# Two layers of a graph network on one core: six buffers for second sigmoids in place of four, nine late load entries in place of ten

## The chip, the cores and the metric

The kernel runs on one core of one Trainium2 chip. The core has five engines that run their own lists of instructions and wait for one another by semaphores: TensorE (PE in the profile; its weight loads are PEld), VectorE (DVE), ScalarE (ACT), GpSimd (POOL) and SyncE (SP), which here issues the loads and stores. The metric is the device time of the program in microseconds, lower is better. The kernel before took 2234.77 us as the median of three runs (2233.01 to 2239.25).

## The reference

`x` is 8192 x 128 and `adj` is 8192 x 8192, all in f32. Layer 0 averages over neighbours; layer 1 weighs every entry of `adj` and of its transpose with a sigmoid of its own:

```python
# layer 0
A = a * adj, with (1 - a) added on the diagonal
x = layernorm(x + relu((A @ x) / A.sum(1) @ W.T + b))
# layer 1
xt  = logmap0(x)
par = adj   * sigmoid((xt @ w_par[:d])[:, None] + (xt @ w_par[d:])[None, :] + b_par)
chi = adj.T * sigmoid((xt @ w_chi[:d])[:, None] + (xt @ w_chi[d:])[None, :] + b_chi)
x = layernorm(x + proj(expmap0(chi @ xt + par @ xt)))
```

Each 8192 x 8192 matrix of scores is thus made once entry by entry, multiplied with `adj`, and consumed by a matmul; none is stored.

## The kernel before, in words

The output is cut into eight panels of 1024 rows. Layer 0 reads `adj` turned, in 256 pairs of tiles (a pair is 128 x 2048, 1 MB), and sums up TensorE products of them. Layer 1 is cut into 512 **units**. Unit n belongs to one panel and one tile of 128 neighbours; it works on 128 x 1024 elements:

- ScalarE makes two sigmoids: the second one, `chi(n)`, into SBUF (L720), and then the first one into a PSUM slot (L737), of which there are three in turn.
- GpSimd multiplies `chi(n)` in place by half of a loaded entry, "nat" (L537, `second_product`).
- VectorE multiplies the PSUM slot by half of another entry, "trn" (L986, `first_product`), and adds the two products into one of three `keys` buffers (L995, `key`).
- TensorE multiplies the keys with the tangent `xtA` (two matmuls of 512 columns, L1180) and sums over the panel's units.

154 units run early, among layer 0's pairs. The other 358 form the **late stage**, which this change touches. Two kinds of units differ there. In an **apart** unit (set `APART`: the unit numbers with n % 8 == 2) the addition is left out: VectorE's product goes straight to `keys`, and TensorE multiplies `keys` (L1180) and `chi` (L1186) one after the other. The buffer of `chi` is then free only when TensorE is done with it, while in all other units it is free when VectorE's addition has read it. In an **own** unit (eight in a row for each of the five panels that end in the late stage) the second matrix is not loaded: TensorE turns the "nat" entries (L1196), and these entries are held until all eight own units are turned.

The order on every engine is written out unit by unit. After a panel's last unit its **final steps** are laid among the next units at fixed distances b + F_...: ScalarE takes out the sums (L760) and squares them (L771), TensorE sums the squares into norms (L1205, just ahead of unit b + 4), ScalarE takes their root (L776; this needs one table load before and one after, because the sigmoids' table is another) ahead of unit b + 7, small steps follow on GpSimd and VectorE, and from b + 14 on ScalarE normalises the panel before, one eighth in each unit (L793). Such steps start at the units 232, 266, 304, 338, 376, 410 and 448; one more root (L781) stands ahead of unit 482.

**Buffers for chi.** `buffer_of` gives three buffers until unit 184 (`MORE`), and from then on four, the fourth in a part of `xA` that layer 0 no longer needs. So `chi(n)` waits until unit n - 4 has let go of its buffer: for `k_ready` (VectorE's addition), or behind an apart unit for `kt_used` (TensorE). The first sigmoid of unit n waits for its PSUM slot, which unit n - 3 held.

**Entries for loads.** SyncE loads 1 MB entries into a ring of seven, and from unit 160 on of ten: three more (`EXTRA`) lie in `xA`. The entries go round in turn, so load i waits for what load i - 10 brought: a "nat" entry is free after GpSimd's second product of the two units, a "trn" entry after VectorE's first product of the two.

Round in this text means the stretch from one own unit to the same one of the next panel, by VectorE's first products: round A is 1493.95 to 1679.68 us, B to 1864.92, C to 2050.11, D (64 units; the others have 72) to 2210.14.

Of the kernel before, what the change touches and what calls it, by code (L numbers as in the profile page):

```python
# [13 lines left out]
BP = 1024  # L14
# [14 lines left out]
CH = 2 * BP  # L29
# [2 lines left out]
PAIRS = NPAN * PPP  # L32
EARLY = 3
RING = 7
EXTRA = 3
CB = 3
KB = 3
SB = 3
PE_LAG = 2
# [133 lines left out]
def load_plan():  # L173
# [10 lines left out]
    for i, (kind, j) in enumerate(kinds):  # L184
        if i == late + RING - 1:
            entries = list(range(RING, RING + EXTRA)) + entries
        e = entries.pop(0)
# [68 lines left out]
MORE = LATE0 + 30  # L256


def buffer_of(n, few):

    if n < MORE:
        return n % few, n - few if n >= few else None
    k = (n - MORE) % (few + 1)
    return (few, n - few - 1 if n > MORE else None) if k == 0 else ((MORE + k - 1) % few, n - few - 1)

# [10 lines left out]
def adj_resnorm_kernel(nc, x_g, xT, g_blk, a_blk, WT, b_row, alpha, w_par, b_par, w_chi, b_chi, out):  # L278
    with ExitStack() as ctx:
        def sb(name, shape):  # L280
            return ctx.enter_context(nc.sbuf_tensor(name, shape, F32))
# [5 lines left out]
        xA = sb("xA", [P, N])  # L287
        xtA = sb("xtA", [P, N])
        acc = sb("acc", [P, EARLY * BP])
        scores = sb("scores", [P, 3, 2, BP])  # L290
        chi_few = sb("chi", [P, CB, BP])
        keys_few = sb("keys", [P, KB, BP])
        dsum = sb("dsum", [P, 2 * BP])
        yb = sb("yb", [P, BP])
        taken = sb("taken", [P, BP])
# [35 lines left out]

        def chi(n):

            b, _ = buffer_of(n, CB)
            return chi_few[:, b, :] if b < CB else xA[:, EXTRA * CH:EXTRA * CH + BP]

        def keys(n):
            return keys_few[:, n % KB, :]


        own_par = [taken[:, :], xA[:, EXTRA * CH + BP:EXTRA * CH + 2 * BP]]

        def natural_of_own(n, k):

# [27 lines left out]
        x_in = [sem(f"x_in{G}") for G in range(NG)]  # L372
        r_in = [sem(f"r_in{e}") for e in range(RING + EXTRA)]
        l_in = [sem(f"l_in{k}") for k in range(3)]
# [238 lines left out]
        def _(act):  # L613
# [93 lines left out]
            def sigmoids(n):  # L707
                k, p, jt = UNIT[n]
                row, c, _ = rows_of(n)
                act.wait_ge(l_in[row], 32 * c)  # L710
                act.wait_ge(prcr_ready, jt // TPP + 1)
                b, before = buffer_of(n, CB)
                if before in APART:
                    act.wait_ge(kt_used, before + 1)
                elif before is not None:
                    act.wait_ge(k_ready, SUMS[before])
                elif b == CB:
                    act.wait_ge(l0_used, PAIRS)
                    act.wait_ge(res_ready, NPAN)
                act.activation(chi(n), scores[:, row, 1, :], ACT.Sigmoid,  # L720
# [11 lines left out]
                else:  # L732
                    s, before = SLOT_OF_UNIT[n]
# [119 lines left out]
            k = NPAN - 1  # L853
# [420 lines left out]
```

## Time and profile before

| | us |
|---|---|
| median of three runs | 2234.77 |
| the profiled execution | 2237.35 |
| its span, first to last instruction | 2235.5 |
| TensorE busy | 2039.8 (91%) |
| VectorE busy | 1935.9 (87%) |
| GpSimd busy | 1334.1 (60%) |
| ScalarE busy | 1326.9 (59%) |

The shares are means over the whole span. In the late stage (from about 1270 us on) the four engines stand closer together, so the stage is read by itself: by its rounds, by who waits for whom in it, and by single places in the timeline. Matmuls are pipelined and their ends are modelled, so TensorE's share is read with care. A wait for several semaphores is put down to the one that came last.

### The profile page before, as it was taken

How to read it: one execution, taken by the hardware profiler on the slowest of the kernel's cores; microseconds unless marked ns; L12 is line 12 of the kernel's file. 1: busy time of each engine (PE TensorE's matmuls, PEld its weight loads, DVE VectorE, ACT ScalarE, POOL GpSimd, SP SyncE). 2: the span in 40 equal slices, each digit the busy share in tenths (PEclk: the TensorE clock that was granted, in tenths of full speed). 3: DMA queues.
4: the chain of work that ended last, by engine and by line, in shares of the span. 5: the costliest groups of instructions: out<-in, count | busy, mean ns of one | idle time of the engine just before them, and what ended most of it. 6: DMA issues, size and time to landing. Idle time of an engine off the chain costs nothing. (4 is left out here: it accounts for less than half of the span.)

```text
span 2235.5 us, 18654 instructions
## 1 busy us (share of the span) xinstructions
PE 2039.8 (91%) x5240; PEld 919.1 (41%) x5240; DVE 1935.9 (87%) x1854; ACT 1326.9 (59%) x1512; POOL 1334.1 (60%) x607
## 2 busy tenths in 40 slices
PE   8999999999999999999999976998888889889886
PEld 3344444444444434444444432343344334334334
DVE  4676878988989988998998988898998998989996
ACT  0011324454454454453453587889888989999996
POOL 0000305435455555643543676999998998999995
PEclk9999999999999999999999988999999999999998
DMA  9998989899889988888888998999999999998992
GB/s 313 333 343 300 387 299 365 361 366 381 361 347 403 405 344 358 347 357 338 369 356 316 421 421 317 384 363 421 421 393 403 421 420 376 421 421 347 421 421 97
DMA packets 129207, 818.29 MB, mean 366 GB/s; under 512 B 14912, under 2 KB 27456, under 8 KB 33360
## 3 DMA queue, kind: packets, MB, share of 16 engines
q1 hardware_dynamic: 122304, 796.97, 89.1%
q10 hardware_dynamic: 6800, 20.13, 2.5%
q8 instruction: 43, 0.70, 0.1%
q14 instruction: 60, 0.49, 0.1%
HBM read 808.59 MB, written 8.45 MB: 365 GB/s over the span
## 5 line engine op out<-in xcount | busy, mean ns | idle before, releaser
L537 POOL TENSOR_TENSOR chi<-chi,ring 128x1024 f32<-128x1024 f32 x323 | 826.9, 2573 | 662.7 <-ACT chi L720 603.5
L1180 PE MATMUL ps<-keys,xtA 128*128 128x512 f32 x2048 | 986.4, 615 | 135.4 <-DVE keys L995 106.1
L1108 PE MATMUL ps<-ring,xA 128*128 128x512 f32 x2048 | 922.5, 600 | 37.9 <-DMA ring<-in_g_blk 33.6
L737 ACT ACTIVATE ps<-scores,prcr 128x1024 f32<-128x1024 f32 x472 | 521.9, 1106 | 389.5 <-DVE keys L995 379.2
L1180 PEld LDWEIGHTS ps<-keys,xtA 128*128 128x128 f32 x2048 | 382.3, 195 | 668.1 <-issue 629.0
L888 DVE TENSOR_TENSOR dsum<-dsum,ring 128x2048 f32<-128x2048 f32 x240 | 593.2, 2472 | 44.7 <-DMA ring<-in_g_blk 37.4
L1108 PEld LDWEIGHTS ps<-ring,xA 128*128 128x128 f32 x2048 | 386.5, 192 | 533.3 <-issue 468.8
L995 DVE TENSOR_TENSOR keys<-ps,chi 128x1024 f32<-128x1024 f32 x395 | 483.7, 1224 | 78.2 <-issue 29.2
L986 DVE TENSOR_TENSOR ps<-ps,ring 128x1024 f32<-128x1024 f32 x381 | 465.9, 1223 | 74.2 <-ACT ps L737 71.1
L720 ACT ACTIVATE chi<-scores,prcr 128x1024 f32<-128x1024 f32 x430 | 488.7, 1137 | 61.0 <-PE ps L1186 45.8
L537 POOL TENSOR_TENSOR chi<-chi,xA 128x1024 f32<-128x1024 f32 x107 | 251.9, 2372 | 32.4 <-ACT chi L720 32.3
L537 POOL TENSOR_TENSOR xA<-xA,ring 128x1024 f32<-128x1024 f32 x49 | 116.2, 2372 | 1.6 <-ACT xA L720 1.6
L995 DVE TENSOR_TENSOR keys<-ps,xA 128x1024 f32<-128x1024 f32 x82 | 100.4, 1225 | 6.6 <-DVE ps L986 2.4
L986 DVE TENSOR_TENSOR ps<-ps,xA 128x1024 f32<-128x1024 f32 x76 | 93.0, 1224 | 14.4 <-ACT ps L737 12.9
L530 POOL TENSOR_TENSOR dsum<-dsum 128x1024 f32<-128x1024 f32 x8 | 18.8, 2354 | 139.6 <-DVE dsum L888 137.2
L720 ACT ACTIVATE xA<-scores,prcr 128x1024 f32<-128x1024 f32 x82 | 93.0, 1134 | 0.4 <-ACT yb L671 0.4
L630 ACT ACTIVATE small<-mv,epsc 128x8 f32<-128x8 f32 x8 | 2.4, 301 | 150.6 <-DVE mv L922 150.6
L537 POOL TENSOR_TENSOR xA<-xA 128x1024 f32<-128x1024 f32 x33 | 78.3, 2374 | 5.0 <-ACT xA L720 5.0
L1186 PE MATMUL ps<-chi,xtA 128*128 128x512 f32 x140 | 65.8, 592 | 0.0
L884 DVE TENSOR_TENSOR dsum<-ring 128x1024 f32<-128x1024 f32 x16 | 34.3, 2182 | 31.8 <-PE ps L1117 17.4
L546 POOL TENSOR_TENSOR acc<-taken,acc 128x1024 f32<-128x1024 f32 x15 | 37.4, 2490 | 31.0 <-ACT taken L753 31.0
L720 ACT ACT_TABLE_LOAD x28 | 35.9, 1283 | 26.8 <-DVE prcr L954 22.6
(109 smaller groups left out, 818.6 us busy)
## 6 DMA issues: line engine op xcount, KB each, us to landing
ring<-in_g_blk SPq DMA_DIRECT2D x461, 1024.0 KB, 10.0
ring<-in_a_cols SPq DMA_DIRECT2D x186, 1024.0 KB, 9.9
xA<-in_a_cols SPq DMA_DIRECT2D x70, 1024.0 KB, 10.9
xA<-in_g_blk SPq DMA_DIRECT2D x31, 1024.0 KB, 12.6
scores<-plcl_d ACTq DMA_DIRECT2D x22, 512.0 KB, 8.1
xA<-in_x_g SPq DMA_DIRECT2D x64, 64.0 KB, 13.4
yb<-in_xT ACTq DMA_DIRECT2D x8, 512.0 KB, 8.8
x_d<-res ACTq DMA_DIRECT2D x8, 512.0 KB, 8.5
```

Of the source, the lines that this page charges most:

```text
L530: pool.tensor_tensor(out=dsum[:, 0:BP], in0=dsum[:, 0:BP], in1=dsum[:, BP:2 * BP], op=ALU.add).then_inc(folded, 1)
L537: pool.tensor_tensor(out=chi(n), in0=chi(n), in1=half(t, n), op=ALU.mult).then_inc(m2_ready, 1)
L546: pool.tensor_tensor(out=at, in0=taken[:, :], in1=at, op=ALU.add).then_inc(acc_added, 1)
L720: act.activation(chi(n), scores[:, row, 1, :], ACT.Sigmoid, bias=prcr[:, 2 * jt + 1:2 * jt + 2]).then_inc(c_ready, 1)
L737: act.activation(dst, scores[:, row, 0, :], ACT.Sigmoid, bias=prcr[:, 2 * jt:2 * jt + 1]).then_inc(p_ready, 1)
L884: dve.tensor_tensor(out=half(dsum, h), in0=half(t0, h), in1=half(t, h), op=ALU.add) \
L888: dve.tensor_tensor(out=dsum[:, :], in0=dsum[:, :], in1=t, op=ALU.add).then_inc(deg_added, 1)
L986: dve.tensor_tensor(out=keys(n) if n in APART else s, in0=s, in1=other, op=ALU.mult).then_inc(m1_ready, 1)
L995: dve.tensor_tensor(out=keys(n), in0=slots[SLOT_OF_UNIT[n][0]], in1=chi(n), op=ALU.add).then_inc(k_ready, 1)
L1108: ins = pe.matmul(Y[:, h * BANK:(h + 1) * BANK], xA[:, tile * D:(tile + 1) * D], t[:, tt * BP + h * BANK:tt * BP + (h + 1) * BANK], start= ...
L1180: ins = pe.matmul(outp[:, h * BANK:(h + 1) * BANK], xtA[:, jt * D:(jt + 1) * D], keys(n)[:, h * BANK:(h + 1) * BANK], start=begins, stop=i ...
L1186: ins = pe.matmul(outp[:, h * BANK:(h + 1) * BANK], xtA[:, jt * D:(jt + 1) * D], chi(n)[:, h * BANK:(h + 1) * BANK], start=False, stop=is_ ...
```

## The change

Unit numbers, the order of the instructions and the work done stay as they are. From unit 184 on there are six buffers for second sigmoids in place of four (three of them in `xA` in place of one), so `chi(n)` waits for unit n - 6. To make room, the late ring has two entries in `xA` in place of three, nine in all, so load i waits for load i - 9.

```diff
--- before.py
+++ after.py
@@ -32,8 +32,9 @@
 PAIRS = NPAN * PPP
 EARLY = 3
 RING = 7
-EXTRA = 3
+EXTRA = 2
 CB = 3
+CB_MORE = 3
 KB = 3
 SB = 3
 PE_LAG = 2
@@ -256,12 +257,13 @@
 MORE = LATE0 + 30
 
 
-def buffer_of(n, few):
+def chi_buffer(n):
 
     if n < MORE:
-        return n % few, n - few if n >= few else None
-    k = (n - MORE) % (few + 1)
-    return (few, n - few - 1 if n > MORE else None) if k == 0 else ((MORE + k - 1) % few, n - few - 1)
+        return n % CB, n - CB if n >= CB else None
+    k = (n - MORE) % (CB + CB_MORE)
+    before = n - CB - CB_MORE
+    return (CB + k, before if before >= MORE else None) if k < CB_MORE else ((MORE + k - CB_MORE) % CB, before)
 
 
 
@@ -331,14 +333,15 @@
 
         def chi(n):
 
-            b, _ = buffer_of(n, CB)
-            return chi_few[:, b, :] if b < CB else xA[:, EXTRA * CH:EXTRA * CH + BP]
+            b, _ = chi_buffer(n)
+            at = EXTRA * CH + (b - CB) * BP
+            return chi_few[:, b, :] if b < CB else xA[:, at:at + BP]
 
         def keys(n):
             return keys_few[:, n % KB, :]
 
 
-        own_par = [taken[:, :], xA[:, EXTRA * CH + BP:EXTRA * CH + 2 * BP]]
+        own_par = [taken[:, :], xA[:, EXTRA * CH + CB_MORE * BP:EXTRA * CH + (CB_MORE + 1) * BP]]
 
         def natural_of_own(n, k):
 
@@ -709,12 +712,12 @@
                 row, c, _ = rows_of(n)
                 act.wait_ge(l_in[row], 32 * c)
                 act.wait_ge(prcr_ready, jt // TPP + 1)
-                b, before = buffer_of(n, CB)
+                b, before = chi_buffer(n)
                 if before in APART:
                     act.wait_ge(kt_used, before + 1)
                 elif before is not None:
                     act.wait_ge(k_ready, SUMS[before])
-                elif b == CB:
+                elif b >= CB:
                     act.wait_ge(l0_used, PAIRS)
                     act.wait_ge(res_ready, NPAN)
                 act.activation(chi(n), scores[:, row, 1, :], ACT.Sigmoid,
```

On ScalarE, around units 412 to 415, where `kt_used` is the wait for TensorE behind the apart unit 410 and L771 is the squares' step. Before:

```order
L720 ACTIVATE chi<-scores,prcr 128x1024 [waits k_ready,prcr_ready,l_in0]
L737 ACTIVATE ps1<-scores,prcr 128x1024 [waits m1_ready]
L771 ACTIVATE dsum<-acc 128x1024 [waits norms_ready,out_evac]
L720 ACTIVATE chi<-scores,prcr 128x1024 [waits kt_used,prcr_ready,l_in0]
L737 ACTIVATE ps0<-scores,prcr 128x1024 [waits k_ready]
L720 ACTIVATE chi<-scores,prcr 128x1024 [waits k_ready,prcr_ready,l_in0]
L737 ACTIVATE ps0<-scores,prcr 128x1024 [waits k_ready]
L720 ACTIVATE xA<-scores,prcr 128x1024 [waits k_ready,prcr_ready,l_in0]
```

After:

```order
L723 ACTIVATE xA<-scores,prcr 128x1024 [waits k_ready,prcr_ready,l_in0]
L740 ACTIVATE ps1<-scores,prcr 128x1024 [waits m1_ready]
L774 ACTIVATE dsum<-acc 128x1024 [waits norms_ready,out_evac]
L723 ACTIVATE xA<-scores,prcr 128x1024 [waits k_ready,prcr_ready,l_in0]
L740 ACTIVATE ps0<-scores,prcr 128x1024 [waits k_ready]
L723 ACTIVATE chi<-scores,prcr 128x1024 [waits k_ready,prcr_ready,l_in0]
L740 ACTIVATE ps0<-scores,prcr 128x1024 [waits k_ready]
L723 ACTIVATE chi<-scores,prcr 128x1024 [waits kt_used,prcr_ready,l_in0]
```

The order stays. The wait for TensorE moves from `chi(414)` to `chi(416)`, and the buffers of more units lie in `xA`.

On SyncE, the loads issued toward the end of round C, where `own_turned` is the wait for the eight own units to be turned. Before:

```order
L513 DMA ring<-in_g_blk 128x2048 [waits m1_ready]
L513 DMA ring<-in_a_cols 128x2048 [waits m2_ready]
L513 DMA ring<-in_g_blk 128x2048 [waits m1_ready]
L513 DMA ring<-in_a_cols 128x2048 [waits own_turned,m2_ready]
L513 DMA ring<-in_g_blk 128x2048 [waits own_turned,m2_ready]
L513 DMA xA<-in_a_cols 128x2048 [waits own_turned,m2_ready]
L513 DMA xA<-in_g_blk 128x2048 [waits own_turned,m2_ready]
```

After:

```order
L516 DMA ring<-in_g_blk 128x2048 [waits m2_ready]
L516 DMA ring<-in_a_cols 128x2048 [waits m1_ready]
L516 DMA ring<-in_g_blk 128x2048 [waits own_turned,m2_ready]
L516 DMA ring<-in_a_cols 128x2048 [waits own_turned,m2_ready]
L516 DMA xA<-in_g_blk 128x2048 [waits own_turned,m2_ready]
L516 DMA xA<-in_a_cols 128x2048 [waits own_turned,m2_ready]
L516 DMA ring<-in_g_blk 128x2048 [waits m2_ready]
```

The loads come in the same order. Each stands behind a wait that belongs to one load later in the ring: the first load that waits for the own units is the fourth row before and the third after, and "nat" loads (`in_a_cols`) now wait for VectorE's products (`m1_ready`), "trn" loads (`in_g_blk`) for GpSimd's (`m2_ready`).

## Rows read from the trace of the kernel before

**Rows 1.** The page: busy time of each engine, transfer rate in 40 slices, and one kind of load.
```profile
PE 2039.8 (91%) x5240; PEld 919.1 (41%) x5240; DVE 1935.9 (87%) x1854; ACT 1326.9 (59%) x1512; POOL 1334.1 (60%) x607
...
GB/s 313 333 343 300 387 299 365 361 366 381 361 347 403 405 344 358 347 357 338 369 356 316 421 421 317 384 363 421 421 393 403 421 420 376 421 421 347 421 421 97
...
ring<-in_a_cols SPq DMA_DIRECT2D x186, 1024.0 KB, 9.9
```

**Rows 2.** Busy time by stretch: one round each; last columns PE clock, DMA share, GB/s.
```profile
1493.95:1679.68 185.73, 161.50 (x437) 73.03 (x436) 170.37 (x189) 165.09 (x166) 172.78 (x88) 0.99 0.99 405
1679.68:1864.92 185.24, 163.18 (x437) 73.74 (x436) 169.97 (x191) 167.39 (x175) 170.56 (x89) 0.98 0.99 407
1864.92:2050.11 185.19, 163.15 (x437) 73.73 (x436) 169.92 (x192) 167.65 (x175) 171.38 (x89) 0.98 0.97 400
2050.11:2210.14 160.03, 140.82 (x373) 61.59 (x372) 148.07 (x150) 146.17 (x152) 150.41 (x74) 1.00 0.89 368
```

**Rows 3.** Waits, 1360 to 2212 us: who waited for whom, us in total, times, longest.
```profile
POOL chi L537 <- ACT chi L720: 60.4, 39, 6.8
ACT chi L720 <- PE ps L1186: 45.8, 26, 2.4
DVE ps L986 <- ACT ps L737: 29.2, 18, 6.2
DVE keys L995 <- POOL chi L537: 16.8, 27, 1.5
```

**Rows 4.** Timeline, ScalarE, round C's first final step: start, length, what, [idle before <-releaser].
```profile
1880.12 1.15 ACT L720 ACTIVATE chi<-scores,prcr 128x1024 f32<-128x1024 f32 x1 [1.88 <-PE ps L1186]
...
1883.58 0.18 ACT L776 ACTIVATE fs<-ps 128x8 f32<-128x8 f32 x1
...
1885.26 1.15 ACT L720 ACTIVATE chi<-scores,prcr 128x1024 f32<-128x1024 f32 x1
```

**Rows 5.** Timeline, TensorE, the same place: the apart unit's second pair, and the norms.
```profile
1878.12 1.88 PE L1186 MATMUL ps<-chi,xtA 128*128 128x512 f32 x4
...
1881.55 1.93 PE L1205 MATMUL ps<-ones,dsum 128*128 128x1 f32 x16
```

**Rows 6.** Timeline, GpSimd, round C: two waits for ScalarE after the first final step.
```profile
1886.55 2.37 POOL L537 TENSOR_TENSOR chi<-chi,xA 128x1024 f32<-128x1024 f32 x1 [2.79 <-ACT chi L720]
...
1904.88 4.84 POOL L537 TENSOR_TENSOR chi<-chi,ring 128x1024 f32<-128x1024 f32 x2 [0.45 <-ACT chi L720]
```

**Rows 7.** Timeline, ScalarE, round C's second final step.
```profile
1962.01 1.15 ACT L720 ACTIVATE chi<-scores,prcr 128x1024 f32<-128x1024 f32 x1 [1.15 <-PE ps L1186]
...
1969.63 0.18 ACT L776 ACTIVATE fs<-ps 128x8 f32<-128x8 f32 x1
```

**Rows 8.** Timeline, TensorE, the same place: the norms.
```profile
1966.88 1.93 PE L1205 MATMUL ps<-ones,dsum 128*128 128x1 f32 x16
```

**Rows 9.** Timeline, VectorE, the same place: the first product that waited.
```profile
1973.57 1.23 DVE L986 TENSOR_TENSOR ps<-ps,ring 128x1024 f32<-128x1024 f32 x1 [1.70 <-ACT ps L737]
```

**Rows 10.** Timeline, ScalarE, round D's late root.
```profile
2126.03 1.15 ACT L720 ACTIVATE chi<-scores,prcr 128x1024 f32<-128x1024 f32 x1 [2.42 <-PE ps L1186]
...
2133.32 1.09 ACT L737 ACTIVATE ps<-scores,prcr 128x1024 f32<-128x1024 f32 x1
```

**Rows 11.** Timeline, VectorE, round D: the sum that frees the slot.
```profile
2130.79 1.22 DVE L995 TENSOR_TENSOR keys<-ps,chi 128x1024 f32<-128x1024 f32 x1
```

**Rows 12.** Timeline, GpSimd, round D: the product behind the late root.
```profile
2138.63 2.37 POOL L537 TENSOR_TENSOR chi<-chi,ring 128x1024 f32<-128x1024 f32 x1 [1.99 <-ACT chi L720]
```

**Rows 13.** Line 513, 1578.0 to 1578.3 us: one load, and its time to landing.
```profile
L513 SPq DMA_DIRECT2D ring<-in_g_blk x1: 328/328/328, 1578.1 to 1578.1; - x1
...
DMA to landing us min/median/max: 14.6/14.6/14.6
```

**Rows 14.** Timeline, VectorE, round A: the product that reads that load.
```profile
1597.14 1.22 DVE L986 TENSOR_TENSOR ps<-ps,ring 128x1024 f32<-128x1024 f32 x1
```

**Rows 15.** Busy time by stretch: the gap in the loads at the end of round C.
```profile
2043.70:2052.60 8.90, 8.90 (x40) 5.56 (x39) 8.76 (x9) 8.48 (x9) 8.90 (x5) 1.00 0.15 44
```

## The prediction

> **What bounds the kernel now.** I read the page first. Over the whole span TensorE and VectorE lead with 91% and 87%, but the change acts on the late stage alone, so these shares decide nothing [rows 1]. The view of busy time by stretch, cut at VectorE's first product of the last own unit, gives the late stage round by round: 185.73, 185.24 and 185.19 us for 72 units each and 160.03 us for the last 64 [rows 2]. In round B VectorE is busy 169.97 us, GpSimd 170.56, ScalarE 167.39, and the transfers move 407 GB/s, where several slices of the page show 421 and none shows more [rows 1, 2]. Four resources are thus within a tenth of the round, and none of them fills it. What is left, some 15 us a round, is hand-over from one to the next.
>
> The view of waits tells which hand-over. From 1360 to 2212 us ScalarE waited 45.8 us, in 26 pieces of up to 2.4 us, for TensorE's L1186, the second pair of matmuls of an apart unit: that is `chi(n + 4)` waiting for the buffer of the apart unit n. GpSimd waited 60.4 us for ScalarE's second sigmoids, and VectorE 29.2 us for first sigmoids and 16.8 us for GpSimd [rows 3]. The change aims at the 45.8 us. They are ScalarE's, though, and not the path's: they count only where the delay reaches GpSimd or VectorE, and where nothing else holds ScalarE at the same place. So the third view is the timeline at such places.
>
> **The wait of chi(n + 4), place by place.** With six buffers `chi(n + 6)` waits for the apart unit. A unit is two sigmoids on ScalarE of about 1.1 us each [rows 4, 10], so n + 6 comes some 4 us after n + 4, more than the longest wait of 2.4 us [rows 3]. I expect the wait to go everywhere but in a stray place. What is late next? ScalarE cannot run further ahead than its PSUM slots let it: the first sigmoid of unit n waits for the addition of unit n - 3. Most of the 26 waits stand where ScalarE is ahead by nearly that much, and removing them makes it wait for a slot instead: worth nothing. Three kinds of places remain where ScalarE has extra work soon after, and VectorE did wait.
>
> First final steps (ahead of unit b + 7 of a panel's first steps). In round C `chi(382)` waited 1.88 us and started at 1880.12; then come a sigmoid, a table load, the root L776 at 1883.58, a table load, and `chi(383)` at 1885.26 [rows 4], for which GpSimd waited 2.79 us [rows 6]. It looks as if 1.88 us came back here. But the root reads the norms that TensorE makes in L1205, from 1881.55 for 1.93 us, so until 1883.48, which is 0.10 us before the root [rows 5]. The profile shows no idle time there because the table load fills it. TensorE's norms stand behind the very L1186 (1878.12 [rows 5]) and are not moved by a buffer of ScalarE's. Take away the wait of 1.88 us and the root still starts at 1883.58. Gain 0 in rounds A, B and C; the bound above is 1.88.
>
> Behind it, GpSimd runs product after product of 2.37 us until it waits 0.45 us for `chi(390)` at 1904.88 [rows 6], which itself waits for an apart unit (386). GpSimd was just set back by 2.79 us, so VectorE follows it here, and the 0.45 us goes: 0.45 us in C, and the same in B, which has the same steps. Round A has no panel before it to normalise at that place, and I count nothing.
>
> Second final steps. `chi(414)` waited 1.15 us; the root L776 started at 1969.63 [rows 7]; the norms were ready at 1966.88 + 1.93 = 1968.81 [rows 8]. So the root can come 0.82 us sooner, less the 0.10 us that passed between norms and root at the first place: 0.72 us. VectorE's first product behind it, at 1973.57, waited 1.70 us for ScalarE [rows 9], so all of the 0.72 us arrives. Three rounds have such a place: 3 x 0.72 = 2.16 us.
>
> The late root (ahead of unit 482, round D). It has no norms to wait for. `chi(478)` waited 2.42 us, and the last first sigmoid before the table load, of unit 481, started at 2133.32 [rows 10]. Its slot is free with the addition of unit 478, at 2130.79 + 1.22 = 2132.01 [rows 11]; with 0.1 us for the hand-over it can start at 2132.1, 1.2 us sooner. GpSimd waited 1.99 us right behind [rows 12], more than 1.2, and is busy from there to the end of the units, so 1.2 us arrives.
>
> Sum of the gains: 2 x 0.45 + 2.16 + 1.2 = 4.3 us. The opening of the late stage (units 184 to 231) I put at 0: there the passage of the last panel sets the pace, and it waits for TensorE, not for a buffer.
>
> **One load entry less.** A load is 1 MB [rows 1], which at 421 GB/s takes 1,048,576 B / 421 GB/s = 2.49 us. With nine entries the loads behind each own stretch are one fewer ahead, so everything lands 2.49 us later against its use. Does anyone then wait? The tightest load I found lies in round A: issued at 1578.1, landed 14.6 us later at 1592.7 [rows 13], used by VectorE at 1597.14 [rows 14]; 4.4 us to spare. 4.4 - 2.49 = 1.9 us remain, and the gain inside a round up to there is at most 0.7. So nobody waits, and the cost is 0. A "trn" load is moreover issued two units later (it now waits for GpSimd's product), 2 x 185.19 / 72 = 5.1 us [rows 2]. Of its 14.6 us to landing most was queue, and the median load of this ring took 9.9 us [rows 1]; 5.1 us later it still reaches a queue that is 2.49 us for each load ahead of it. That is covered as long as two loads stand ahead. If the cover fails, a "trn" load costs up to 5.1 us less 4.4, so 0.7 us a round.
>
> The gap in the loads while own units are turned (share 0.15 from 2043.70 to 2052.60 [rows 15]) begins one load sooner. It is idle time of the transfers and counts only if they bind. They bound no round: full rate would have moved round B's bytes in 185.24 x 407 / 421 = 179.1 us, A's in 178.7, C's in 175.9 [rows 2]. This also caps what the buffers can give: 7.1 + 6.2 + 9.3 us in the three rounds.
>
> The Trainium skill, DMA: Bandwidth & Descriptors, Specifications, gives a limit of about 358 GB/s from HBM for one core. By that rule the transfers would bind every round, and the buffers would be worth nothing. The trace disagrees: rounds A to C ran at 400 to 407 GB/s [rows 2].
>
> Operations on the moved buffers keep their shapes; a product that reads `xA` and one that reads the ring both took 2.37 us [rows 6, 12]. I take 0.
>
> **The sum.** The profiled execution took 2237.35 us, its span 2235.5. The span becomes 2231.2 and the execution 2233.1. The median of the runs is 2.6 us below the profiled one, so the forecast is 2234.77 - 4.3 = 2230.5 us. What a measurement of this kernel can tell from no change is about 0.3%, 6.7 us: the forecast lies inside.
>
> **Rivals.**
> The waits were on the path. If the norms do not hold the root (because TensorE's own work also comes sooner once GpSimd and VectorE do), the first final steps give 1.88 us in A, B and C, the second ones 1.15 each: 5.64 + 3.45 + 0.9 + 1.2 = 11.2 us, 2223.6 us. For it: GpSimd's wait of 2.79 us and VectorE's behind it. Against: 0.10 us between norms and root. With the transfers' cap the far end is 22.6 + 1.2 = 24 us, 2211 us, which needs every hand-over to shrink.
>
> Nothing arrives. VectorE and GpSimd are so close to each other that what one gains the other holds: 2234.8 us. The rule of the Trainium skill above gives this time too.
>
> The ring starves (the slower side). The mechanism: the transfers, not the engines, set the rounds, and each gap at an own stretch (four: before A, and after A, B and C) grows by one load of 2.49 us, which is never made up: 10.0 us, 2244.8 us, the gains being lost too. For it: 400 to 407 of 421 GB/s, and the gap of [rows 15]. Against: 4.4 us between landing and use at the tightest place. It decides from the point where that spare falls under 2.49 us plus the gain.
>
> **Chances.** The forecast's mechanism (gain of 2 to 6.7 us) 0.48, own range 2228 to 2233; on the path 0.27; nothing arrives 0.15; starving 0.10. Faster than 0.3%: 0.27 and a little of the first, 0.29. Slower: most of the starving case, 0.09. Within: 0.62. The range runs from 2221 to 2239 us; it leaves out the far end of the second case and most of the last.
>
> **What would show it.** ScalarE's wait for L1186 falls from 45.8 us to under 5, and its waits for VectorE's additions grow in its place. In each first final step the root still starts 0.1 us behind the norms. The second final step's wait of VectorE falls from 1.70 to about 1.0 us. Rounds: A 185.0, B and C 184.1, D 158.8. No first or second product waits for a load; the smallest spare between landing and use is 1 to 2 us. The prediction is wrong if rounds fall below 183 us (the norms did not hold), if a wait for a load shows up on GpSimd or VectorE, or if the waits of GpSimd for ScalarE stay at 60 us.

## The result, and the profile after

The kernel after took 2248.27 us (median of 10 runs, 2245.28 to 2251.68), the kernel before in the same comparison 2234.7 (10 runs, 2228.63 to 2241.34). The ratio is 1.006, with a 95% interval of 1.0049 to 1.0072: **slower by 13.6 us**, a small difference but clear of the noise. Forecast were 2230.5 us, with a range of 2221 to 2239 and a chance of 0.09 for slower. The forecast was wrong in its sign, and the time lies outside its range.

The profiled execution of after took 2251.67 us, its span is 2249.9, so 14.4 us more than before. First the stretches of [rows 2], cut at the same units, from the view of busy time by stretch (columns as there):

```profile
1493.81:1684.06 190.25, 165.69 (x437) 75.01 (x436) 170.29 (x190) 165.23 (x166) 170.89 (x87) 0.96 0.96 394
1684.06:1873.25 189.19, 163.20 (x437) 73.47 (x436) 170.37 (x191) 168.27 (x175) 171.34 (x89) 0.98 0.97 399
1873.25:2058.32 185.07, 162.74 (x437) 73.72 (x436) 169.90 (x191) 168.28 (x175) 171.31 (x89) 0.98 0.97 400
2058.32:2223.37 165.05, 143.52 (x373) 63.31 (x372) 148.18 (x149) 145.83 (x152) 149.62 (x74) 0.98 0.88 363
```

A lost 4.5 us, B 4.0, C nothing, D 5.0. VectorE's and GpSimd's busy times are unchanged to within 2 us, so this is waiting. Where in a round? I cut each round once more. The **own stretch** goes from VectorE's first product two units ahead of the first own unit to that of the last own unit (nine units); the rest is the **ordinary stretch**. Of before, rounds A and B, ordinary and own in turn:

```profile
1494.00:1656.30 162.30, 139.88 (x341) 59.23 (x340) 148.40 (x171) 144.45 (x147) 150.14 (x79) 0.99 1.01 417
1656.30:1679.70 23.40, 21.59 (x97) 13.79 (x96) 21.94 (x21) 20.61 (x20) 22.62 (x10) 1.00 0.79 326
1679.70:1843.30 163.60, 141.60 (x341) 59.95 (x340) 148.64 (x173) 147.26 (x156) 148.92 (x80) 0.98 1.01 419
1843.30:1864.90 21.60, 21.54 (x97) 13.79 (x96) 21.29 (x20) 20.09 (x20) 21.60 (x10) 1.00 0.78 319
```

The same of after, and below them the own stretches of its rounds C and D:

```profile
1493.80:1655.90 162.10, 141.20 (x341) 59.72 (x341) 148.27 (x171) 146.87 (x149) 148.90 (x78) 0.98 1.01 418
1655.90:1684.10 28.20, 24.53 (x97) 15.29 (x96) 22.07 (x21) 18.42 (x18) 22.04 (x10) 0.88 0.62 257
1684.10:1846.90 162.80, 140.05 (x341) 59.01 (x340) 148.31 (x172) 149.87 (x158) 149.32 (x80) 0.99 1.01 419
1846.90:1873.20 26.30, 23.05 (x97) 14.42 (x96) 22.02 (x20) 18.32 (x18) 21.93 (x10) 0.94 0.69 279
...
2036.10:2058.30 22.20, 21.52 (x97) 13.79 (x96) 21.51 (x19) 18.30 (x18) 21.95 (x10) 1.00 0.62 258
...
2194.00:2223.40 29.40, 25.06 (x97) 15.63 (x98) 22.00 (x20) 16.47 (x16) 22.02 (x10) 0.88 0.29 116
```

Two things are to be seen. The ordinary stretches became shorter, by 0.2 to 1.3 us each. The whole loss of the four rounds lies in the own stretches: 23.4 to 28.2, 21.6 to 26.3, 21.6 to 22.2, 23.1 to 29.4, together 16.4 us. And in a good own stretch TensorE is busy 21.54 of 21.60 us: TensorE bounds it, while in the ordinary stretch of B it is busy 141.60 of 163.60 us.

Next the waits, 1360 to 2226 us, which answer to [rows 3]:

```profile
POOL xA L540 <- ACT xA L723: 44.0, 20, 6.8
POOL chi L540 <- ACT chi L723: 37.7, 25, 5.3
ACT ps L740 <- DVE keys L998: 28.1, 60, 2.6
...
DVE ps L989 <- PE ps L1199: 18.5, 33, 3.4
...
PE ps L1199 <- DMA ring<-in_a_cols: 9.4, 6, 3.2
...
PE ps L1199 <- DMA xA<-in_a_cols: 3.9, 2, 3.2
```

ScalarE's 45.8 us for the second pair are gone, as meant: no row has ScalarE waiting for L1189, the line that was L1186. New is a chain that the prediction never names: TensorE's L1199 (the turning of own entries, L1196 before) waits 13.3 us for loads, and VectorE 18.5 us for L1199. One place of it, TensorE at the head of round A's own units, before and then after:

```profile
1658.02 0.64 PE L1196 MATMUL ps<-ident,ring 128*128 128x128 f32 x4
1660.47 0.51 PE L1196 MATMUL ps<-ident,ring 128*128 128x128 f32 x2 [1.81 <-DMA ring<-in_a_cols]
1660.82 1.88 PE L1180 MATMUL ps<-keys,xtA 128*128 128x512 f32 x4
```

```profile
1657.40 0.63 PE L1199 MATMUL ps<-ident,ring 128*128 128x128 f32 x4
1658.46 0.51 PE L1199 MATMUL ps<-ident,ring 128*128 128x128 f32 x2 [0.43 <-DMA ring<-in_a_cols]
1662.20 0.70 PE L1199 MATMUL ps<-ident,xA 128*128 128x128 f32 x2 [3.24 <-DMA xA<-in_a_cols]
1662.70 3.62 PE L1183 MATMUL ps<-keys,xtA 128*128 128x512 f32 x4
1666.11 1.49 PE L1199 MATMUL ps<-ident,ring 128*128 128x128 f32 x6
```

These rows hold the cause. **The first own unit does not read one load but four.** `turn_own(n)` makes eight transposes, two from each of the four "nat" entries of the eight own units (`natural_of_own` returns entry `(OWN[...] + k) // 2` for k from 0 to 7). And the loop on TensorE calls `turn_own(n + 2)` ahead of `products(n)`. So the fourth entry, which GpSimd needs only at the seventh own unit, is needed by TensorE two units before the first own unit. Even before, TensorE waited there: 1.81 us in A, 1.03 in D. In B the fourth load landed 0.9 us after the turn began and just in time for its last two transposes; in C it landed 1.2 us ahead of the turn, 1.9 us ahead of those two. After, the waits in A to D were 0.43 + 3.24, 3.25, 0.68 and 0.20 + 1.99 + 1.97 us; another 1.52 us stand in the own stretch ahead of round A.

The second thing in the rows: the four matmuls behind the wait took 3.62 us in place of 1.88, and the next turn's six transposes 1.49. The granted clock, by stretch, after:

```profile
1658.00:1662.20 4.20, 0.54 (x3) 0.31 (x2) 2.76 (x3) 1.26 (x2) 4.20 (x3) 0.86 1.00 421
1662.20:1666.10 3.90, 3.90 (x6) 1.74 (x7) 2.46 (x2) 1.89 (x2) 2.07 (x1) 0.50 1.03 435
```

The clock fell to its lower level, 1.2 GHz (0.50), toward the end of the idle time (the mean of 0.86 over the 4.20 us before says that it was low for some 1.2 us of them), and stayed there while TensorE worked, in the one stretch that TensorE bounds. VectorE paid in two pieces:

```profile
1662.94 1.23 DVE L989 TENSOR_TENSOR ps<-ps,taken 128x1024 f32<-128x1024 f32 x1 [2.15 <-PE ps L1199]
...
1668.06 1.23 DVE L989 TENSOR_TENSOR ps<-ps,xA 128x1024 f32<-128x1024 f32 x1 [2.63 <-PE ps L1199]
```

So round A's 4.8 us split into idle time of TensorE, (28.2 - 24.53) - (23.4 - 21.59) = 1.9 us, and the same work at a lower clock, 24.53 - 21.59 = 2.9. In B it is 3.2 and 1.5, in C 0.7 and 0, in D 3.1 and 3.2.

**The account of the span.** Own stretches of A to D +16.4 us, ordinary ones -3.1, last product to the end +1.1 (26.5 after, 25.4 before; the other runs spread from 24.7 to 26.6, so I read nothing into it), start of round A -0.1. Sum 14.3, measured 14.4. The -0.1 hides two things that cancel: the own stretch ahead of round A grew from 21.8 to 23.6 us, by the same wait, and it began 1.9 us sooner. Over all traces its beginning spreads from 1467.6 to 1473.5 us, so the second is no effect that can be read.

### The profile page after: what moved, and what is told of

Its sections match the earlier page's. It is cut to its first block, busy times and chain, and to the rows that moved or that the text cites. A ratio compares the mean times of both kernels' runs of the same rounds, so it can differ in the third digit from the quotient of the medians.

```text
span 2249.9 us, 18656 instructions
## 1 busy us (share of the span) xinstructions
PE 2046.6 (91%) x5240; PEld 926.4 (41%) x5240; DVE 1938.1 (86%) x1854; ACT 1329.5 (59%) x1512; POOL 1334.3 (59%) x607
## 4 chain that ended last, share of the span: by engine, by line
PE 41%; POOL 18%; issue 14%; DVE 12%; ACT 8%; DMA 6%; ACTq 0%; DVEq 0%; SPq 0%; POOLq 0%
PE ps L1111 26%; POOL chi L540 11%; PE ps L1183 11%; POOL xA L540 6%; DVE dsum L891 4%; DVE ps L989 3%; DMA ring<-in_g_blk 3%; ACT chi L723 2%; DMA ring<-in_a_cols 2%; ACT ps L740 2%; PE ps L1199 2%; ACT xA L723 1%; DMA xA<-in_a_cols 1%; DVE keys L998 1%; POOL acc L549 1%
## 5 line engine op out<-in xcount | busy, mean ns | idle before, releaser
L540 POOL TENSOR_TENSOR chi<-chi,ring 128x1024 f32<-128x1024 f32 x298 | 768.2, 2592 | 659.1 <-ACT chi L723 601.2
L740 ACT ACTIVATE ps<-scores,prcr 128x1024 f32<-128x1024 f32 x472 | 522.9, 1108 | 412.8 <-DVE keys L998 400.0
L989 DVE TENSOR_TENSOR ps<-ps,ring 128x1024 f32<-128x1024 f32 x373 | 455.9, 1222 | 83.5 <-ACT ps L740 80.9
L998 DVE TENSOR_TENSOR keys<-ps,chi 128x1024 f32<-128x1024 f32 x334 | 409.0, 1224 | 68.9 <-issue 33.8
L723 ACT ACTIVATE chi<-scores,prcr 128x1024 f32<-128x1024 f32 x347 | 394.1, 1136 | 15.5 <-DMA scores<-plcl_d 8.3
L540 POOL TENSOR_TENSOR xA<-xA,ring 128x1024 f32<-128x1024 f32 x136 | 319.6, 2371 | 42.2 <-ACT xA L723 42.2
L998 DVE TENSOR_TENSOR keys<-ps,xA 128x1024 f32<-128x1024 f32 x143 | 175.1, 1225 | 14.4 <-POOL xA L540 6.5
L723 ACT ACTIVATE xA<-scores,prcr 128x1024 f32<-128x1024 f32 x165 | 187.2, 1135 | 0.0
L540 POOL TENSOR_TENSOR chi<-chi,xA 128x1024 f32<-128x1024 f32 x49 | 115.5, 2369 | 19.9 <-ACT chi L723 19.9
L540 POOL TENSOR_TENSOR xA<-xA 128x1024 f32<-128x1024 f32 x29 | 68.4, 2372 | 1.9 <-ACT xA L723 1.8
L1199 PEld LDWEIGHTS ps<-ident,ring 128*128 128x128 f32 x256 | 37.8, 207 | 27.3 <-issue 16.5
```

Of the source, the lines that this page charges most:

```text
L540: pool.tensor_tensor(out=chi(n), in0=chi(n), in1=half(t, n), op=ALU.mult).then_inc(m2_ready, 1)
L723: act.activation(chi(n), scores[:, row, 1, :], ACT.Sigmoid, bias=prcr[:, 2 * jt + 1:2 * jt + 2]).then_inc(c_ready, 1)
L740: act.activation(dst, scores[:, row, 0, :], ACT.Sigmoid, bias=prcr[:, 2 * jt:2 * jt + 1]).then_inc(p_ready, 1)
L989: dve.tensor_tensor(out=keys(n) if n in APART else s, in0=s, in1=other, op=ALU.mult).then_inc(m1_ready, 1)
L998: dve.tensor_tensor(out=keys(n), in0=slots[SLOT_OF_UNIT[n][0]], in1=chi(n), op=ALU.add).then_inc(k_ready, 1)
L1199: ins = pe.transpose(columns(slots[s], k), columns(half(t, h), UNIT[n][2] % TPP), ident[:, :])
```

## Experiments

Each run was compared with the kernel before on the same chip (2235.3, 2235.84 and 2235.64 us in the three batches). "Own stretches" lists those of A, B, C, D as defined above; before has 23.4, 21.6, 21.6, 23.1, after 28.2, 26.3, 22.2, 29.4. The stretches come from each run's profiled execution.

### The two halves apart

**ring9**: the kernel before with nine entries and nothing else.

```diff
-EXTRA = 3
+EXTRA = 2
```

> The kernel before with nine late entries and its four buffers: the ring's half of the change alone. Theory 1 (the turn of the first own unit needs the fourth own load, and one entry less makes that load late): the whole loss is here, and the buffers only took a little of it back. The own stretches of rounds A, B and D get 4.7 to 6.3 us longer, C under 1, and the rest keeps its length: 16 us in all, 2251 us. Theory 2 (the loss comes with the six buffers, by ScalarE running ahead): 2235 us, as before. Theory 3 (loads are late everywhere): about 2248, but with the loss spread over each round's ordinary units.

Measured: 2251.05 us (4 runs), ratio 1.007 (1.0055 to 1.0085), as theory 1 had it. The whole loss is the ring's. Its stretches in round A, ordinary and own:

```profile
1495.96:1658.34 162.38, 139.99 (x341) 59.28 (x341) 148.48 (x171) 144.29 (x147) 149.28 (x78) 0.99 1.01 418
1658.34:1685.10 26.76, 23.33 (x97) 14.44 (x96) 21.99 (x20) 20.52 (x20) 22.58 (x10) 0.94 0.66 271
```

The ordinary stretches of all rounds stand within 0.1 us of before's. Own stretches 26.8, 24.2, 21.6, 28.2. ScalarE's wait for L1186 is 45.9 us, as before. TensorE's waits for loads, 1360 to 2226 us:

```profile
PE ps L1196 <- DMA ring<-in_a_cols: 6.8, 5, 2.6
PE ps L1196 <- DMA xA<-in_a_cols: 3.2, 1, 3.2
```

**chi5_ring10**: ten entries, and as many buffers as then fit, five. The second of the two places for the first sigmoids of own units moves to `sqT`, the part of `dsum` that holds the squares, and ScalarE waits for it until the norms are made. The edit in its main lines; the function `chi_buffer` of the kernel after comes with it:

```diff
+CB_MORE = 2
-        own_par = [taken[:, :], xA[:, EXTRA * CH + BP:EXTRA * CH + 2 * BP]]
+        own_par = [taken[:, :], sqT]
...
+                        if i % TPP == 1:
+                            act.wait_ge(norms_ready, sum(b < n for _, b in FINALS))
```

> Ten entries, and five buffers for second sigmoids: the fifth stands where the kernel before held every second first sigmoid of own units, which moves into the half of dsum that holds squares. The buffers' half of the change nearly alone. Theory 1: ScalarE's wait for L1186 falls from 45.8 us to under 10, and the kernel gains about 3 us: 2231.5 us. Theory 2 (the buffers do the harm): 2240 us or more.

Measured: 2234.25 us (10 runs), 0.9997 (0.9987 to 1.0007): no change that shows, 2.7 us above the expectation. A fifth buffer does nearly all that the sixth does: ScalarE's 45.8 us fall to 3.3, and the ordinary stretches shorten by 0.2, 0.7, 0.7 and 1.2 us (2.8 together; after has 0.2, 0.7, 0.8 and 1.3). But the own stretches became 23.3, 22.4, 21.6 and 24.3, 1.9 us more than before's. TensorE's waits for the loads, of this kernel:

```profile
PE ps L1201 <- DMA ring<-in_a_cols: 2.6, 2, 1.7
...
PE ps L1201 <- DMA xA<-in_a_cols: 2.0, 1, 2.0
```

The fourth load comes no sooner when the units ahead of it go faster, so TensorE waits longer for it: in B the load landed 0.7 us later against VectorE's product at that place than in before, in D 1.2 us, about what the units ahead had gained. What the buffers gain in B and D is given back at the end of the round; C, where 1.9 us were to spare, keeps its 0.7.

### Is it the four loads in one turn?

**after_own1** and **before_own1**: the transposes of an own unit read that unit's own load alone. The number of instructions stays, but the turned tile is another one, so these two kernels no longer compute the reference; they tell only what the need for four loads costs.

```diff
-            return loaded("nat", (OWN[OWN_AT[n] // TPP * TPP] + k) // 2), k % 2
+            return loaded("nat", n // 2), k % 2
```

> The changed kernel, but each own unit's turn reads its own load eight times in place of all four own loads (so the turned tile is another; the amount of work is the same). The turn of the first own unit then needs the first own load alone. Theory 1: the waits of TensorE for loads in the own stretches go, rounds A, B and D fall back by 4.7 to 6.3 us each, and the kernel takes about 2232 us, a little less than before. Theory 3 (loads late everywhere): no more than a few us are won, 2244 us.

> The same edit in the kernel before (each own unit turns from its own load alone). Theory 1: TensorE's waits of 1.8 and 1.0 us for the fourth own load in rounds A and D go, and what follows them: 3 us in all, 2231 to 2232 us. Against the same edit in the changed kernel this gives the six buffers by themselves: theory 1 has them worth 0 to 3 us; a theory in which they cost something has this kernel the faster one by 3 us or more.

Measured: after_own1 2231.41 us (10 runs), 0.9983 (0.9973 to 0.9992); before_own1 2231.57 (10 runs), 0.9988 (0.9977 to 1.0). With the same ring of nine entries the 13.6 us are gone, and after_own1 is no slower than before. Own stretches 21.6, 21.6, 21.6, 21.8 in both. Round A in after_own1, TensorE:

```profile
1657.81 1.11 PE L1199 MATMUL ps<-ident,ring 128*128 128x128 f32 x8
1658.95 1.96 PE L1183 MATMUL ps<-keys,xtA 128*128 128x512 f32 x4
```

Nothing waits here, neither for loads nor at a lower clock. This pair also tells what the buffers give when the ring costs nothing: 2231.57 against 2231.41, nothing that shows, though the four rounds together are 2.2 us shorter in the trace (712.2 and 710.1); the intervals, some 2 us to either side, leave room for both. And before itself paid for the four loads: 3.7 us by the medians, with an interval that just reaches no change, and 3.1 us in the own stretches of the traces.

**ring8**: before with eight entries.

```diff
-EXTRA = 3
+EXTRA = 1
```

> The kernel before with eight late entries and its four buffers. Theory 1: the fourth own load is late by one load more, 2.5 us, in every own stretch, with what follows from it: 4 to 5 us more a round than with nine entries, and now in round C too, where nine cost nothing; the ordinary stretches (162.4, 163.6, 163.6 and 136.9 us) stay within 1 us, but for round A, whose tightest ordinary load had 4.4 us to spare and loses 5.0. In all 2266 us. If the loss with nine entries came from something else than how many loads stand ahead (the new pairing of waits), eight entries, which pair as ten do, take less than 2251.

Measured: 2267.42 us (4 runs), 1.0142 (1.0127 to 1.0157). Own stretches 28.1, 29.4, 26.0, 30.0. C, which one entry less had nearly left alone, is hit now: its spare was 1.9 us, less than one load. The own stretch ahead of round A, not in this list, went from 21.8 to 27.1. The ordinary stretches still stand within 0.9 us of before's. Eight entries pair the waits as ten do and cost more than nine, so the new pairing of the waits in after was not the cause.

### Turning one unit later

**after_turn1**, **before_turn1** and **chi5_ring10_turn1**: the load is given one more unit of time.

```diff
-                if n + 2 in OWN_AT:
-                    turn_own(n + 2)
+                if n + 1 in OWN_AT:
+                    turn_own(n + 1)
```

> The changed kernel, but TensorE turns an own unit one unit later: ahead of the products of the unit before it, in place of two units before. The first own unit's need for the fourth own load then comes 2.4 us later, the time of one unit, and nothing else of the ring or the buffers changes. Theory 1 (this need sets the loss): the waits of 3.2 us for that load in rounds A and B shrink to about 0.8, and the own stretches, now 28.1, 26.3, 22.2 and 29.4 us in rounds A to D, fall to some 24, 23.5, 22 and 26: 2238 us. If the late turn itself hinders the own units (VectorE has to wait for the turned tile), they are at 24 us everywhere.

> The kernel before with the same later turn. Theory 1: its two waits for the fourth own load (1.8 us in round A, 1.0 in D) go, 2231.5 us, as with each unit turned from its own load. If the late turn hinders, the own stretches grow over 21.6 us and the kernel is at 2236 or above.

> Ten entries, five buffers for second sigmoids and the later turn together. With five buffers alone the ordinary units gained 2.8 us and the own stretches gave back 1.9 of it, by waits of 1.75, 0.8 and 1.97 us for the fourth own load. Theory 1: the later turn covers all three waits, so the buffers' gain arrives: 2229 us, against 2231.5 with the later turn alone.

Measured: 2247.45 us, 1.0056 (1.0041 to 1.0071); 2247.9, 1.0056 (1.0038 to 1.0075); 2246.08, 1.0049 (1.0034 to 1.0065); 4 runs each. **All three times expected by theory 1 missed, by 9 to 17 us;** the other branch that two of the expectations name, that the late turn itself hinders, is what happened. The part on the loads held in A to C: TensorE's longest waits in A and B fell from 3.24 and 3.25 to 1.42 and 0.72 us, and C's went. In D of after_turn1 0.82 + 1.98 us of waiting stayed, with the lower clock behind it. Its own stretches are 26.7, 26.0, 25.0 and 29.9, those of chi5_ring10_turn1 25.0, 25.0, 25.0 and 25.7. But the later turn has a price that I had put at nearly nothing. In before_turn1 TensorE waits for no own load at all, and still every own stretch takes 25.0 us, 3.4 more than the 21.6 of a good one. TensorE and then VectorE in its round A, and the own stretch as a whole:

```profile
1661.97 1.96 PE L1180 MATMUL ps<-keys,xtA 128*128 128x512 f32 x4 [0.98 <-DVE keys L995]
1663.76 0.39 PE L1196 MATMUL ps<-ident,xA 128*128 128x128 f32 x2
```

```profile
1664.91 1.23 DVE L986 TENSOR_TENSOR ps<-ps,taken 128x1024 f32<-128x1024 f32 x1 [0.69 <-PE ps L1196]
```

```profile
1659.35:1684.30 24.95, 23.93 (x101) 14.45 (x99) 22.00 (x20) 20.82 (x21) 22.95 (x10) 1.00 0.69 281
```

TensorE bounds the own stretch, so its first turn has to be made while VectorE still sets the pace. Here TensorE idles 0.98 us before the first turn, and the stretch holds 101 of its matmuls in place of 97, the products of one unit more: 23.93 us busy against 21.54. The two together are the 3.4 us. VectorE then waits for the turns; its waits for the turns, 1360 to 2226 us, are one for each of the 40 own units in the five stretches, 2.6 us a stretch (in before there are 12 of them, 2.1 us in all):

```profile
DVE ps L986 <- PE ps L1196: 13.2, 40, 0.7
```

### Splitting the first turn

**after_split** and **before_split**: the first own unit's turn starts where it did, but its second half, which reads the third and fourth load, comes behind the products of unit n.

```diff
-            def turn_own(n):
+            def turn_own(n, part=range(TPP)):
...
+                begins = OWN_AT.get(n + 2, 1) % TPP == 0
                 if n + 2 in OWN_AT:
-                    turn_own(n + 2)
+                    turn_own(n + 2, range(4) if begins else range(TPP))
                 products(n)
+                if begins:
+                    turn_own(n + 2, range(4, TPP))
```

> The changed kernel, with the first own unit's eight transposes in two parts: the four that read the first two own loads stay in place, the four that read the third and fourth come behind the products of the unit between. The other seven units are turned as before, so nothing but the first unit's need for the late loads moves, by about 2.4 us; the later turn of all units had cost 25.0 us in every own stretch and hidden this. Theory 1: the waits of 3.2 us in rounds A and B shrink to about 0.8 and 1.3, C's 0.7 goes, and the own stretches fall from 28.1, 26.3, 22.2 and 29.4 to about 24.5, 22.5, 21.6 and 26.5 us: 2237 us. If the need for the fourth load is not what costs, nothing changes: 2248.

> The kernel before with the first own unit's turn in two parts. Theory 1: both of its waits (1.8 us in round A, 1.0 in D) are covered and all own stretches take 21.6 to 21.8 us: 2232 us, as when each unit turned from its own load.

Measured: after_split 2239.33 us (10 runs), 1.0019 (1.001 to 1.0029); before_split 2234.66 (10 runs), 0.9992 (0.9981 to 1.0002). The split brings after 9 us back, against 11 expected; before_split is 2.7 us above its expectation and not to be told from before. TensorE in round A of after_split:

```profile
1660.13 1.95 PE L1183 MATMUL ps<-keys,xtA 128*128 128x512 f32 x4 [0.51 <-DVE keys L998]
...
1664.24 0.51 PE L1200 MATMUL ps<-ident,xA 128*128 128x128 f32 x2 [1.93 <-DMA xA<-in_a_cols]
```

The load still comes 1.93 us late, but TensorE has done its products meanwhile, and the clock stays up. The own stretches are 24.2, 23.8, 22.0, 26.7. In before_split all are 22.0: the split itself costs up to 0.5 us a stretch against 21.6, which is a part of why before gains less than expected.

**after_split_store** and **chi5_split_store**: the loads need 2.5 us each, but the fourth own load landed 3.7 to 3.8 us behind the third in rounds A to C, because a store of 0.5 MB is issued between them. `F_STORE` puts it behind the fourth.

```diff
-F_STORE = 36
+F_STORE = 38
```

> The changed kernel with the turn in two parts, and with the store of a finished panel (0.5 MB) issued one load later, behind the fourth own load in place of ahead of it. Theory 1: the fourth own load lands 1.25 us sooner in rounds A, B and C (not in D, which has no store there). With the split turn no wait is left in A, B and C, and D keeps its 26.5 us: 2235 us, about the kernel before.

> Ten entries, five buffers for second sigmoids, the turn in two parts and the later store. Theory 1: no own stretch waits for a load (21.6 us in A to C, up to 22.5 in D), and the ordinary stretches keep the buffers' gain (162.2, 162.9, 162.9 and 135.7 us): 2230 us, faster than both kernels by 0.2% and more. If the buffers' gain were given back elsewhere it would stay at 2232, the time of the split turn alone.

Measured: after_split_store 2237.79 us (10 runs), 1.0003 (0.9992 to 1.0014), own stretches 22.7, 22.6, 22.0, 25.2. The fourth load now lands 2.5 us behind the third in A to C, and the wait for it in A fell from 1.93 to 0.45 us, but not to nothing as expected, and the time is 2.8 us above the expectation. D has no store there and still became 1.5 us shorter than in after_split: its waits are the same, but the clock stayed up (last section).

chi5_split_store (ten entries, five buffers, the split turn and the later store together) 2232.19 us (12 runs, 2228.36 to 2235.82), **0.9986 (0.9977 to 0.9995)**: the lowest median of this study among the kernels that compute the reference, 3.5 us under before and 16 under after, but its interval overlaps that of before_split. It is 2.2 us above its expectation, and at the 2232 that the expectation gave for the case in which the buffers' gain is given back; the stretches speak against that case. Of TensorE's waits for own loads one is left:

```profile
PE ps L1202 <- DMA xA<-in_a_cols: 0.4, 1, 0.4
```

Its own stretches are 22.0, 22.0, 22.0, 22.7, and the ordinary ones keep the buffers' gain (162.2, 162.9, 162.9 and 135.6). Against before_split the four rounds are only 1.2 us shorter, though (712.3 and 713.5); the part on the gains in the next section says why.

## Why the prediction was wrong, point by point

**The step that failed** is "One load entry less": "The tightest load I found lies in round A ... 4.4 us to spare ... So nobody waits, and the cost is 0." The size of the shift was about right: in A to D the fourth own load landed 2.1 to 3.7 us later against VectorE's product of the unit at which it is turned, a load being 2.49. Wrong was the place. I had looked for the tightest load where units read loads one by one, and VectorE's and GpSimd's use in the timeline gave 4.4 us [rows 13, 14]. The consumer that reads four loads at once, ahead of its units, was TensorE's L1196. At its place before had no spare but a deficit in A and D (1.81 and 1.03 us), none in B and 1.9 us in C. The trace of before says so, in the 24th row of its waits from 1450 to 2200 us:

```profile
PE ps L1196 <- DMA ring<-in_a_cols: 1.8, 1, 1.8
```

TensorE's waits for loads there sum to less than 3 us, so a list sorted by size puts them far down, and I read only its top. The cost was 16.4 us in the own stretches of A to D, not 0.

**"They bind no round" was read from too long a stretch.** 407 of 421 GB/s in round B [rows 2] is a mean of two regimes: 419 GB/s at a share of 1.01 for 163.6 us, and 319 at 0.78 for the 21.6 us of the own stretch. In the ordinary stretch the transfers are full, and a gain of the engines there came out of the spare of the turn's fourth load (chi5_ring10: 2.8 gained, 1.9 given back). The spare of the "trn" loads is another matter: in round A of before it is 17.8 us at unit 232, 4.5 at unit 272 and 8.0 at unit 288, so the tightest of them told nothing about the turn. They still don't set the ordinary stretch itself: ring9 and ring8 leave its length as it was, and after_own1 runs A to C in 184.4 us or less with nine entries. The limit of 358 GB/s that the prediction cites from the Trainium skill, DMA: Bandwidth & Descriptors, Specifications, stays contradicted by these rows.

**The slower rival** ("the ring starves", 10.0 us, chance 0.10) had the sign and nearly the size, and its deciding point, a spare under 2.49 us, was right as a sentence. Its mechanism was not: each gap was to cost one load, evenly. The loss was 4.8, 4.7, 0.6 and 6.3 us, it comes through one instruction of TensorE, and 7.6 of its 16.4 us are TensorE's lower clock, which no case of mine had. I gave it 0.10 on the strength of the 4.4 us.

**The gains** in the trace of after, place by place, from VectorE's first products in both traces, counted from each round's start:

| place | forecast | measured |
|---|---|---|
| first final steps, root | 0 | 0.06 us sooner |
| behind them (units 387 to 395), B, C | 0.45 each | 0.6 each |
| second final steps, A, B, C | 0.72 each | 0.09 each |
| late root, D | 1.2 | 1.25 |

The second row has a reason that the prediction did not know. At that place TensorE has waited for the sums to be taken out and then makes twelve matmuls ahead of the apart unit's second pair, for which ScalarE's `chi(390)` waits with four buffers. Round C of before, and then of before_split, which has four buffers too:

```profile
1894.64 7.11 PE L1180 MATMUL ps<-keys,xtA 128*128 128x512 f32 x12 [2.31 <-ACT acc L765]
```

```profile
1893.60 5.42 PE L1180 MATMUL ps<-keys,xtA 128*128 128x512 f32 x12 [2.32 <-ACT acc L765]
```

In the first the granted clock was at its lower level for 3.4 us, in the second it stayed at 1.00, and ScalarE then waited 2.28 and 0.58 us. In the six traces with four buffers there are twelve such places in B and C: seven with the lower clock, where ScalarE waited 2.1 to 2.3 us, and five without, where it waited 0.6. With five or six buffers it never waits there, whatever the clock does. So the 0.6 us are what the buffers save where the clock falls; in B and C of before_split, where it does not, the ordinary stretches are 163.0 us without any further buffer, 0.1 to 0.2 above those with them.

The first row held by its reason too: in round C of after ScalarE now waits openly for the norms, which end at 1889.88 + 1.93 = 1891.81, 0.04 us before the root:

```profile
1889.88 1.93 PE L1208 MATMUL ps<-ones,dsum 128*128 128x1 f32 x16
```

```profile
1891.85 0.18 ACT L779 ACTIVATE fs<-ps 128x8 f32<-128x8 f32 x1 [1.90 <-PE ps L1208]
```

The second final steps failed as a step. ScalarE there, round C of after, answers to [rows 7]:

```profile
1974.76 1.12 ACT L740 ACTIVATE ps<-scores,prcr 128x1024 f32<-128x1024 f32 x1 [1.35 <-DVE keys L998]
1975.90 1.28 ACT L779 ACT_TABLE_LOAD   x1
1977.19 0.18 ACT L779 ACTIVATE fs<-ps 128x8 f32<-128x8 f32 x1
```

The wait of 1.15 us for the buffer has turned into one of 1.35 us for the PSUM slot, ahead of the last first sigmoid (L740) before the table load. That is the rule which the prediction states in general ("removing them makes it wait for a slot instead: worth nothing") and then did not apply at this place. At the late root I did work out the slot, and that number held. The root comes 0.77 us sooner in the round (1977.19 - 1873.25 against 1969.63 - 1864.92), but 0.68 of it had been gained earlier in the round. Together the stretches gained 3.0 us, forecast 4.3, of which 1.2 are the second row's and hang on the clock.

**The signs that I named**: ScalarE's wait for TensorE under 5 us: yes, and its waits for additions took the place (7.6 us before, 28.1 after). VectorE's wait of 1.70 us at the second final step, to fall to about 1.0: it is 1.60, as the third row of the table would have it. GpSimd's waits for ScalarE staying at 60 us would mean wrong: they did not fall. A product in `xA` has its own row, so the sums are 60.4 + 6.6 = 67.0 us before and 37.7 + 44.0 = 81.7 after; in ring9, with the old buffers, they are 78.1, so most of the growth is the ring's. The smallest spare of an ordinary load, forecast 1 to 2 us, is 2.2. "No product waits for a load": true as written, and the gap in it, TensorE's turn, is the whole result.

## What to carry to other kernels

Before taking an entry from a ring, list every instruction that waits for a load, on every engine, and for one that needs several at once take the last of them at the time of that instruction. A small existing wait for a load (here 1.8 us) says that the spare is already negative there, and is worth more than the busy shares; look for it at the bottom of the list of waits too. Cut rates at the places where the ring is held: a mean of 407 of 421 GB/s hid a stretch that ran full and a gap, and while it ran full the engines' gain came out of the spare of the next load that was waited for. And before a few tenths of a us are put down to an edit, look at the granted clock at the place in both traces.

## What the runs showed of the hardware that I had not expected

TensorE's wait for a load costs more than its length once the clock falls in it. In own stretches a wait of 1.81 us (before, A), of 1.93 (after_split, A) and of 2.62 (ring9, B) left the granted clock at 1.00; in ring9 the own stretch, 24.2 us, was longer by just the 2.6. With waits of 2.81 us (ring8, C) and 3.24 us (after, A) the clock went to its lower level; ring8's own stretch in C is 26.0 us long at a mean clock of 0.93. TensorE behind the wait in ring9's round B and in ring8's round C:

```profile
1854.11 1.88 PE L1180 MATMUL ps<-keys,xtA 128*128 128x512 f32 x4
```

```profile
2053.73 3.39 PE L1180 MATMUL ps<-keys,xtA 128*128 128x512 f32 x4
```

So 0.2 us more of waiting went with 1.8 us more of own stretch. In round D of after two waits of 1.99 and 1.97 us with two transposes between them had the same effect (clock 0.50 behind them, and the four matmuls 3.62 us). The Trainium skill, TensorE: Matmul & The Clock Gate, HAM oscillation, tells of a kernel whose matmuls start each tile slow because the wait for a DMA lets the clock drop; the trace agrees, with the rows above.

The length of the wait alone does not decide it. The two rows of twelve matmuls above stand behind waits of 2.31 and 2.32 us, one with the lower clock and one without. The same is true of round D in after_split and in after_split_store, with waits of 0.25, 0.26 and 1.97 us in the one and 0.31, 0.27 and 1.95 in the other:

```profile
2196.50 2.38 PE L1200 MATMUL ps<-ident,ring 128*128 128x128 f32 x10 [1.97 <-DMA ring<-in_a_cols]
```

```profile
2193.01 1.47 PE L1200 MATMUL ps<-ident,ring 128*128 128x128 f32 x10 [1.95 <-DMA ring<-in_a_cols]
```

Over the 3.6 us from there on the granted clock is 0.53 in the first and 1.00 in the second, and the own stretches are 26.7 and 25.2 us. No run here shows what decides between the two, so a wait of this size is to be priced both with and without the lower clock. The cost depends on what bounds the place: here it is the one stretch of the round in which TensorE has no slack.
